# An FFN output bias as a product of ones on TensorE instead of an addition by GpSimd

## What is computed

```python
def _L0_ffn_ref(x, gate_W, gate_b, wi_W, wi_b, wo_W, wo_b, lora_A, lora_B):
    top1 = jnp.argmax(jax.nn.softmax(x @ gate_W.T + gate_b, axis=-1), axis=-1)
    base = jnp.einsum('bsd,fd->bsf', x, wi_W) + wi_b
    out = jnp.zeros_like(x)
    for i in range(8):
        lora = jnp.einsum('bsr,fr->bsf', jnp.einsum('bsd,rd->bsr', x, lora_A[i]), lora_B[i])
        inter = jax.nn.relu(base + lora)
        expert_out = jnp.einsum('bsf,df->bsd', inter, wo_W) + wo_b
        out = out + (top1 == i)[..., None] * expert_out
    return out
x = x + 0.5 * ffn(layernorm(x))
x = x + attn(layernorm(x))        # xLSTM scan over time, then silu(h@w_gate)*(h@w_up)@w_down
x = x + 0.5 * ffn(layernorm(x))
```

## Time and profile before

| | |
|---|---|
| median of 3 runs | 901.93 us (900.47 to 907.58) |
| the profiled execution | 905.12 us, with a span of 902.9 us from its first to its last instruction |
| instructions | 30704 |
| TensorE clock granted, mean | 0.989 of full speed |

### The profile page before, as it was taken

How to read it: one execution, slowest core, us unless ns; L and a number is a source line. 1 busy time by engine, 2 the same in 40 slices (tenths; PEclk the granted TensorE clock), 3 DMA queues, 4 the chain that set the end, 5 groups by cost and what they waited for, 6 DMA issues and landing times.

```text
span 902.9 us, 30704 instructions
## 1 busy us (share of the span) xinstructions
PE 847.1 (94%) x12744; PEld 814.7 (90%) x12744; DVE 621.4 (69%) x1502; ACT 358.9 (40%) x716; POOL 247.9 (27%) x234
## 2 busy tenths in 40 slices
PE   2998679999899998999899999999999989999998
PEld 2998569999799998999889998999989979999998
DVE  5665586686757778486766868668585898797642
ACT  4545242534424443343523435244352462234421
POOL 2102335220432114311323214323044133612100
PEclk9999889999999999999999999999999999999999
DMA  9203654202434013412315412531133154520000
GB/s 241 92 25 86 160 159 129 63 25 60 115 108 119 13 49 95 127 50 65 80 46 147 108 34 69 150 105 33 29 112 107 43 132 132 139 69 2 1 25 24
DMA packets 96265, 76.03 MB, mean 84 GB/s; under 512 B 11935, under 2 KB 84767, under 8 KB 96129
## 3 DMA queue, kind: packets, MB, share of 16 engines
q1 hardware_dynamic: 96128, 74.08, 30.1%
HBM read 56.75 MB, written 17.30 MB: 82 GB/s over the span
## 4 chain that ended last, share of the span: by engine, by line
PE 68%; issue 7%; DVE 4%; POOL 2%; SPq 2%; DMA 2%; ACT 1%; POOLq 0%; DVEq 0%; ACTq 0%
PE bank L1124 19%; PE bank L1125 18%; PE bank L1126 18%; PE bank L1160 3%; PE bank L1271 2%; PE bank L1331 1%; PE bank L1310 1%; PE bank L1350 1%; DMA parts_scratch<-pc 1%; PE bank L1285 1%; PE bank L1365 1%; SPq L481 1%; POOL pc L581 1%; DMA arena<-parts_scratch 1%; PE bank L1374 1%
## 5 line engine op out<-in xcount | busy, mean ns | idle before, releaser
L669 ACT ACTIVATE r_h<-bank 128x512 fp32r<-128x512 f32 x128 | 76.5, 598 | 215.4 <-PE bank L1160 152.9
L1124 PE MATMUL bank<-xT_hi,wi_hi 128*128 128x256 f32 x512 | 147.1, 287 | 1.9 <-DVE r_l L861 1.4
L1124 PE MATMUL bank<-wo_hi,r_h 128*128 128x256 f32 x512 | 146.7, 287 | 0.0
L1125 PE MATMUL bank<-wo_hi,r_l 128*128 128x256 f32 x512 | 143.6, 281 | 0.0
L1126 PE MATMUL bank<-xT_lo,wi_hi 128*128 128x256 f32 x512 | 143.6, 281 | 0.0
L1125 PE MATMUL bank<-xT_hi,wi_lo 128*128 128x256 f32 x512 | 143.6, 281 | 0.0
L1126 PE MATMUL bank<-wo_lo,r_h 128*128 128x256 f32 x512 | 143.6, 280 | 0.0
L861 DVE SCALAR_TENSOR_TENSOR r_l<-bank,r_h 128x512 fp32r<-128x512 f32 x128 | 87.7, 685 | 73.2 <-ACT r_h L669 73.0
L1124 PE MATMUL bank<-xT_hi,wgu_hi 128*128 128x256 f32 x352 | 101.7, 289 | 0.0
L1124 PEld LDWEIGHTS bank<-xT_hi,wi_hi 128*128 128x128 f32 x512 | 96.9, 189 | 4.0 <-DVE r_l L861 2.3
L1126 PE MATMUL bank<-xT_lo,wgu_hi 128*128 128x256 f32 x352 | 98.3, 279 | 0.0
(11 more groups left out here) (157 smaller groups left out, 2124.2 us busy)
## 6 DMA issues: line engine op xcount, KB each, us to landing
dm<-f_scratch SPq DMA_DIRECT2D x128, 128.0 KB
arena<-parts_scratch SPq DMA_DIRECT2D x96, 128.0 KB
arena<-parts_scratch SPq DMA_DIRECT2D x96, 64.0 KB
arena<-parts_scratch SPq DMA_DIRECT2D x32, 192.0 KB
x<-in_x SPq DMA_DIRECT2D x16, 256.0 KB, 3.0
parts_scratch<-pa SPq DMA_DIRECT2D x32, 128.0 KB
parts_scratch<-pb SPq DMA_DIRECT2D x32, 128.0 KB
parts_scratch<-pc SPq DMA_DIRECT2D x32, 128.0 KB
```

The lines of the kernel that those rows point to most:

```text
L669: nc.scalar.activation(flat(r_h[:, n]), U[use % 2][:], ACT.Relu).then_inc(f_rh, 1)
L1124: nc.tensor.matmul(dst, lh, rh, start=first, stop=False, **more)
L1125: nc.tensor.matmul(dst, ll, rh, start=False, stop=False, **more)
```

## The change

The addition by POOL and its semaphore go away. In the down-projection's sum, before the first of a half's products, PE makes two more products, one for each tile of the half: the weights are rows 96 and 97 of u_st (ones), the moving operand is rows 96 and 97 of a new tile bias_o, with the high part of wo_b in the one and the remainder in the other. They open the sum (start=True), and L900 halves them with the rest. POOL's step keeps its letter in the order, but does nothing there.

At the start, ACT makes the high part (2x256), DVE takes the remainder in both rows, and ACT writes the high part again over row 96. half_wo_b is not made any more; y may be written once both ACT copies are done.

```diff
-        half_wo_b = sb("half_wo_b", [P, D])
+        bias_o = sb("bias_o", [P, D], F32R)
@@ GpSimd, stream G
                     if r.ffn:
-                        if r.i == 0:
-                            pool.wait_ge(s_half, 1)
-                        pool.wait_ge(g_xn, TILES * (r.i + 1))
-                        bias = half_wo_b[:].unsqueeze(1).to_broadcast([P, TILES, D])
-                        nc.gpsimd.tensor_tensor(xb, xb, bias, ALU.add).then_inc(g_xb, 1)
+                        yield
+                        continue
@@ ScalarE, stream H
                         act.wait_ge(s_bias, 16)
-                        nc.scalar.mul(half_wo_b[:], wo_b, 0.5).then_inc(s_half, 1)
+                        nc.scalar.copy(bias_o[LS:LS2], wo_b[LS:LS2]).then_inc(s_half, 1)
+                        act.wait_ge(s_bias_lo, 1)
+                        nc.scalar.copy(bias_o[LS:LS + 1], wo_b[LS:LS + 1]).then_inc(s_half, 1)
@@ VectorE, stream H
                         v.tensor_tensor(hi[ER:2 * ER], stage[ER:2 * ER], hi[ER:2 * ER].bitcast(F32), ALU.subtract).then_inc(w_lo, 1)
+                        dve.wait_ge(s_half, 1)
+                        v.tensor_tensor(bias_o[LS:LS2], wo_b[LS:LS2], bias_o[LS:LS2].bitcast(F32), ALU.subtract).then_inc(s_bias_lo, 1)
@@ VectorE, end of a half
                     if r.ffn:
-                        dve.wait_ge(g_xb, r.k + 1)
+                        dve.wait_ge(g_xn, TILES * (r.i + 1))
                         v.scalar_tensor_tensor(to, T[:], 0.5, to, ALU.mult, ALU.add).then_inc(f_fin, 1)
@@ VectorE, stream Y
-                        dve.wait_ge(s_half, 1)
+                        dve.wait_ge(s_half, 2)
@@ TensorE, stream V
                         if p == 0:
                             pe.wait_ge(f_fin, 2 * r.d + h)
+                            if r.ffn:
+                                if r.k == 0:
+                                    pe.wait_ge(s_half, 2)
+                                for jj in range(2):
+                                    nc.tensor.matmul(T[:, jj * D:(jj + 1) * D], u_st[LS:LS2, 0:P], bias_o[LS:LS2], start=jj == 0, stop=False,
+                                                     skip_group_check=True)
...
-                                                   f == 0 and jj == 0, f == 2 * r.pairs - 1, skip_group_check=True)
+                                                   not r.ffn and f == 0 and jj == 0, f == 2 * r.pairs - 1, skip_group_check=True)
```

More of the change, by code:

```diff
@@ L284, in build @@
         s_ident, s_route, s_bias, s_const = sig("ident_loaded"), sig("route_loaded"), sig("bias_loaded"), sig("const_loaded")
+        s_bias_lo = sig("bias_remainder_done")
         s_setup, s_half, s_zero = sig("setup_done"), sig("half_bias_done"), sig("values_cleared")
@@ L292, in build @@
         g_sq = sig("g_sq")
-        g_xn, g_xb, g_xr = sig("g_xn"), sig("g_xb"), sig("g_xr")
+        g_xn, g_xr = sig("g_xn"), sig("g_xr")
         g_tr, g_hi, g_x32, g_lo = sig("g_tr"), sig("g_hi"), sig("g_x32"), sig("g_lo")
```

## The result

| | before | after |
|---|---|---|
| median | 902.65 us (4 runs, 900.47 to 907.58) | 928.84 us (4 runs, 926.64 to 930.32) |
| ratio, 95% interval | | 1.0286 (1.0261 to 1.0312) |
| span of the profiled execution | 902.9 us | 927.6 us |
| mean granted clock | 0.989 | 0.985 |
| PE busy, products | 847.1 us, 12744 | 869.6 us, 12808 |

A forecast was written before the change was run, and what follows sets the result against it. PE was taken as the bound. Products 7.5, seam 10.6 and start 1.2, less POOL's relief 1.5 and hidden 2.0, gave +15.8 us on the 901.93 median: 917.7 us, range 906 to 925.

The forecast's parts named there:

- PE bounds the kernel: From 140 us on PE is busy 97%, so a microsecond more on PE is nearly one more of time.
- The 64 products at 0.117: The added bias products on PE take 0.117 us each, their 2 rows saving nothing: 7.5 us in all.
- The seam: Stepping into and out of the 32-row strip on PE costs 0.33 us for each of 32 pairs, 10.6 us.
- The row that I leaned on: Narrow 32-column strips at L1310 on PE: 0.78 us around 32 products, read as 0.25 us lost going in and out.
- Rival A: The step into and out of the strip on PE is free: +5.2 us, 907 us; chance 0.20.
- about 0.8: Expected us on PE from the last product before a pair to the second whole-array one after; ideally 0.47.
- rival C: Entering and leaving the strip each drain PE, 0.42 us a pair, nothing hidden or returned: +22.1, 924 us; chance 0.12.
- Hidden, 2 us: PE's existing waits shorten when PE arrives later, absorbing 2 us of the added work, between 0 and 4.
- The sign to look for: PE idle between 140 us and the end stays near 23 us, the span growing by about the cost of 32 pairs.
- which I had feared for: The granted clock, 0.88 from 84 to 140 us, could fall once more; not in rival C's sum.
- POOL's relief, 1.5 us: Dropping POOL's addition shortens PE's waits for c_ex by 1.5 us, between 0 and 3.3.
- The start, 1.2 us: DVE's new subtraction waits for ACT's copy, routing products come 1.55 us later, and 1.2 us is lost by the transposes.

The follow-up runs named there:

- the whole-array pair: Changed kernel with the 64 added products on 98 rows from row 0 instead of the 2-row strip: 916.42 us, ratio 1.0155.
- the second pair: Changed kernel with the two strip products issued twice for each half, so the bias comes in twice: 939.96 us, ratio 1.0408.
- The kernel with waits for pairs: Changed kernel with the added products replaced by eight waits for something long done at each of 32 places: 910.60 us, ratio 1.0085.
- the shift by 80: Kernel before, work untouched, with 80 more wait-only instructions ahead of PE's first step: 917.75 us, ratio 1.0140.
- those by 128 and 192: Kernel before, work untouched, with 128 or 192 more wait-only instructions ahead of PE's first step: 919.80 and 919.32 us, ratios 1.0180 and 1.0181.

## Why the prediction missed, step by step

- **PE bounds the kernel: right.** From 140 us on PE's added work came back as time, nearly one for one.
- **The 64 products at 0.117: right.** 0.114 to 0.12 each, by the whole-array pair and the second pair. 7.5 us.
- **The seam: right in kind, too small.** It came as a loss on the way in and out, as at the narrow strips, but 0.40 us and not 0.33; 32 x 0.07 = 2.2 us more. The row that I leaned on lumps going in and out with 32 products whose own time I put at its ceiling of 0.30, and any time taken off there belongs to the seam. The chosen value's own bounds, 0.25 to 0.36, were narrower than the 0 to 0.42 worked out above them. (0.25 + 0.09 is also 0.34 and not 0.33, which is 0.3 us over 32 pairs.) Rival A is out; the distance of "about 0.8" was 0.87, nearer to rival C's 0.9.
- **Hidden, 2 us: about right in size, not shown in cause.** The sign to look for, idle time near 23 us after 140 us, came out at 25.6, but 5.8 us of new stalls are in that. PE's waits for named releasers went from 10.3 to 7.3 us, so 3.0 us less. The kernel with waits for pairs, which has no work there, has 7.7, and the one without pairs 10.1; so the stalls may have hidden them as well as the pairs, and single traces scatter by a microsecond or two. The mean clock from 84 to 140 us, which I had feared for, is 0.88 as in the earlier trace rows. From 140 us on the granted clock is at the lower of its two levels for 13.6 us (before the last product) instead of 6.8, which costs up to 3.4 us and had no term.
- **POOL's relief, 1.5 us: wrong.** 0.5 us, within the measurement's uncertainty of none. An addition that "may stand ahead of c_ex" did not: nothing in the rows had put it there.
- **The start, 1.2 us: right.** The timeline of all engines after:

```profile
14.49 1.22 DVE L838 TENSOR_TENSOR lora_b<-k,lora_b 32x1024 fp32r<-32x1024 f32 x1
...
16.30 0.40 ACT L645 CAST bias_o<-y 2x256 fp32r<-2x256 f32 x1
...
16.73 0.42 DVE L840 TENSOR_TENSOR bias_o<-y,bias_o 2x256 fp32r<-2x256 f32 x1 [1.02 <-ACT bias_o L645]
17.18 0.69 DVE L1011 TENSOR_TENSOR xT_lo<-bank,xT_hi 128x512 fp32r<-128x512 f32 x1
...
19.73 0.19 DVE L1025 TENSOR_TENSOR won<-lg,lmax 128x32 f32<-128x32 f32 x1
...
21.87 0.54 PE L1300 MATMUL bank<-ident,u_rep 128*96 128x128 f32 x3
```

  The whole start lies 1.5 us earlier here than in the earlier trace rows for reasons outside the change, so I read distances. From the subtraction on lora_b (14.49; 15.99 before) to the remainder for routing are 2.69 us instead of 1.24: +1.45, where 1.55 was said. DVE waits 1.02 us for ACT and then takes its 0.42. POOL's addition is gone from beside L1025, which takes 0.19 instead of 1.04. To the transposes at L1300 it is 7.38 us instead of 6.30: +1.1.
- **The step that wasn't there.** This is the step that failed. The sum had no term for PE's own supply of instructions, and gave no reason for leaving it out. It moved by +5.8 us, more than the seam and the relief were off by together. The waits of before already had 8.2 us of it, and the page's chain 7% "issue". Adding 128 instructions to PE, loads included, at 32 places moves every later one against the places where PE can run dry.

Together: seam +2.2, relief +1.0 and stalls +5.8 are 9.0 us over the forecast's +15.8, or +24.8 against 26.2 measured. Two smaller terms work against each other: 1.0 us more hidden than said, and up to 3.4 us of lower clock, for +23.8 to +27.2. (The table above leaves both out.) Without the stalls the same terms give +19 and some 921 us, inside the range; it is they that took the time above it. Rival C, with 0.65 us a pair and nothing hidden, ended at 924. It too lacked the stalls.

## What to carry to other kernels

A pair of products on a strip of few rows between whole-array ones is paid for on the way in and out, 0.40 us here; fill the rows with zeros from row 0 on until it covers the whole array, as the 98 rows did here (where between 34 and 98 the border lies, and whether few rows that start at row 0 would pay, wasn't tried), or put the bias into rows that a whole-array product already has, as the input bias of this kernel does. When PE is the bound, costs are set by starts around the place and not by durations or rows. Where the chain shows "issue" on a PE that works in dense narrow products, an edit that adds or removes PE instructions moves the time by their number alone, here by up to 1.4% (the shift by 80; those by 128 and 192 reach 1.8%, with a later first product in it): try a shifted variant before reading a difference below that as the edit's own.

## What was not expected of the hardware

- Waits alone, ahead of the first product, change the time of identical work from 902.2 to 903.3 us (before, in these groups) to 905.3, 916.1, 917.8, 919.8 and 919.3 us. With 128 and 192 of these instructions the first product starts at 15.88 and 22.77 us: 0.11 us each. Up to 80 of them leave the first product where it was, at 9.3 to 10.7 us.
- PE stands still for 0.3 to 3.4 us in and just behind dense narrow stretches, at places that repeat about every 128 products and move with the number of instructions. It goes on 1.2 to 1.7 us after a 16 KB packet of the instruction queue has landed.
- A half and a quarter of the array's rows, both away from row 0, cost the same to enter and leave; 98 rows from row 0 cost nothing. Inside the part loads go ahead of products as usual.
